# A recurrent block with routed experts on one core: smaller zero rows and prefetch before the slots, and a reordered first step

## What is computed

```
x = x + layernorm(attn(layernorm(x)))     # token shift, k/v/r projections, the wkv recurrence,
                                          # output projection, then a channel mix of width 1024
x = x + layernorm(ffn(layernorm(x)))

def wkv step(aa, bb, pp; k, v):           # per channel, along the tokens
    p  = max(pp, u + k);  y  = (exp(pp-p)*aa + exp(u+k-p)*v) / (exp(pp-p)*bb + exp(u+k-p))
    p2 = max(pp + w, k);  aa = exp(pp+w-p2)*aa + exp(k-p2)*v;  bb = exp(pp+w-p2)*bb + exp(k-p2)

def ffn(x):
    idx = argmax(x @ Wg)                  # one of 8 experts for each token
    return geglu(x, shared weights) + geglu(x, W1[idx], W2[idx], W3[idx])
```

## Time and profile before

| | |
|---|---|
| median of 3 runs | 1000.21 us (999.18 to 1000.51) |
| profiled execution | 1001.62 us, its span 999.7 us |
| TensorE busy | 924.4 us, 92% |
| VectorE busy | 725.1 us, 73% |
| GpSimd busy | 591.2 us, 59% |
| ScalarE busy | 586.2 us, 59% |
| chain that ended last | TensorE 64%, VectorE 11%, GpSimd 8%, no visible wait 7% |
| DMA | 152.09 MB, mean 152 GB/s |

### The profile page before, as it was taken

The page is one execution under the profiler, slowest core; times in us unless marked ns, Lnnn a source line. Parts: engine busy times, 40 slices in busy tenths (PEclk is TensorE's granted clock), DMA queues, the critical chain, the costliest instruction groups (busy, mean ns, idle before and its releaser), DMA issues.

```text
span 999.7 us, 27993 instructions
## 1 busy us (share of the span) xinstructions
PE 924.4 (92%) x9734; PEld 836.7 (84%) x9734; DVE 725.1 (73%) x1651; ACT 586.2 (59%) x1014; POOL 591.2 (59%) x800
## 2 busy tenths in 40 slices
PE   2477999999999999999999999869999999999994
PEld 1366888888888889888888878769999999999994
DVE  6999999999999999999999985614444444444442
ACT  5487768868868868869778755313333333333340
POOL 5475766866866866866866441434455555555553
PEclk9699999999999999999999999989999999999998
DMA  7033152152253153163171263936787778576410
GB/s 240 13 107 112 48 212 79 71 212 70 81 212 105 42 218 97 42 221 94 42 254 53 86 211 128 336 132 188 232 273 250 232 250 273 171 245 216 159 56 21
DMA packets 82091, 152.09 MB, mean 152 GB/s; under 512 B 5423, under 2 KB 62896, under 8 KB 76914
## 3 DMA queue, kind: packets, MB, share of 16 engines
q1 hardware_dynamic: 34528, 72.39, 21.1%
q10 hardware_dynamic: 42944, 61.98, 19.2%
q0 software_dynamic: 4560, 16.98, 4.4%
HBM read 183.59 MB, written 46.25 MB: 230 GB/s over the span
## 4 chain that ended last, share of the span: by engine, by line
PE 64%; DVE 11%; POOL 8%; issue 7%; ACTq 4%; DMA 3%; ACT 3%; SPq 1%; POOLq 0%; DVEq 0%
PE up L366 12%; PE up L368 12%; PE up L367 12%; PE yp L366 6%; PE yp L368 6%; PE yp L367 6%; PE yp L572 2%; PE yp L575 2%; PE tp L375 2%; ACTq L940 2%; PE yp L588 2%; DVE arena L1026 2%; POOL mix_s L1608 1%; DVE er L1127 1%; POOL routed_rows L1641 1%
## 5 line engine op out<-in xcount | busy, mean ns | idle before, releaser
L366 PE MATMUL up<-mix_s,arena 128*128 128x128 f16 x1248 | 211.9, 219 | 0.3 <-DVE ex L1474 0.2
L367 PE MATMUL up<-mix_s,arena 128*128 128x128 f16 x1248 | 211.8, 219 | 0.0
L368 PE MATMUL up<-mix_s,arena 128*128 128x128 f16 x1248 | 211.8, 219 | 0.0
L366 PE MATMUL up<-xf_s,arena 128*128 128x256 f16 x512 | 139.5, 272 | 1.5 <-issue 1.5
L1707 POOL TENSOR_TENSOR kf_s<-ex,kf_s 128x512 f16<-128x512 f32 x78 | 90.2, 1156 | 85.6 <-ACT kf_s L986 85.5
L368 PE MATMUL up<-xf_s,arena 128*128 128x256 f16 x512 | 139.5, 273 | 0.0
L367 PE MATMUL up<-xf_s,arena 128*128 128x256 f16 x512 | 139.5, 272 | 0.0
L1474 DVE SCALAR_TENSOR_TENSOR ex<-up,ex 128x512 f32<-128x512 f32 x78 | 53.9, 691 | 102.6 <-ACT ex L980 102.5
L366 PEld LDWEIGHTS up<-mix_s,arena 128*128 128x128 f16 x1248 | 122.4, 98 | 1.3 <-DVE ex L1474 1.2
L367 PEld LDWEIGHTS up<-mix_s,arena 128*128 128x128 f16 x1248 | 122.4, 98 | 0.4
L368 PEld LDWEIGHTS up<-mix_s,arena 128*128 128x128 f16 x1248 | 122.4, 98 | 0.0
(11 more groups left out here) (226 smaller groups left out, 2865.6 us busy)
## 6 DMA issues: line engine op xcount, KB each, us to landing
arena<-w_split ACTq DMA_DIRECT2D x113, 1024.0 KB
arena<-in_W SPq DMA_DIRECT2D x24, 1024.0 KB, 6.5
w_split<-arena SPq DMA_DIRECT2D x24, 1024.0 KB, 9.2
rows<-routed_rows ACTq DMA_DIRECT2D x39, 261.0 KB, 2.8
arena<-w_split SPq DMA_DIRECT2D x9, 1024.0 KB
normed<-routed_rows ACTq DMA_DIRECT2D x37, 128.0 KB, 2.5
x_in<-in_x SPq DMA_DIRECT2D x16, 256.0 KB, 2.8
x_res<-in_x SPq DMA_DIRECT2D x16, 256.0 KB, 2.8
```

Of the source, the lines that this page charges most:

```text
L366: pe.matmul(out, stat(0), mov(0), start=first, stop=False)
L367: pe.matmul(out, stat(0), mov(1), start=False, stop=False)
L368: return pe.matmul(out, stat(1), mov(0), start=False, stop=last)
```

## The change

In the passage: the zero tile has 520 columns (`ID`) in place of 780. SyncE writes the last 260 columns of all eight zero blocks before the first slots, and the first 520 of all eight behind them, under a semaphore of their own, for which ScalarE waits at the end of slot 0. ScalarE issues no zeros. Slot 1's up weights aren't prefetched; they are loaded once, without a condition, behind slot 1's rows, and TensorE's count for them is lower by one load. In the head: in step 0 the first exponential stands ahead of `above(1)`, and keep times values goes to `delta2`, a tile that is free in that step, without a wait for the last relu pieces. The low halves of pieces 4 and 5 move from step 1 to step 0, before `kept`, and that of piece 6 from `own(4)` to `own(3)` of step 1.

```diff
-        zero_row = ex.rearrange("p n k c -> p (n k c)")[:, 2 * CT * CH:2 * CT * CH + ROW]
+        zero_row = ex.rearrange("p n k c -> p (n k c)")[:, 2 * CT * CH:2 * CT * CH + ID]
...
-        OWN_LO = {(-2, 0): (0, 3), (-1, 1): (3, 4), (1, 3): (4, 6), (1, 4): (6, 7), (2, 3): (7, 8), (2, 0): (8, 9)}
+        OWN_LO = {(-2, 0): (0, 3), (-1, 1): (3, 4), (0, 4): (4, 6), (1, 3): (6, 7), (2, 3): (7, 8), (2, 0): (8, 9)}
...
-                for e in range(E // 2):
+                for e in range(E):
                     at = sp.value_load(end_at[0:1, e:e + 1], min_val=0, max_val=E * REGION - P)
-                    sp.dma_start(routed_rows[bass.ds(at, P)], zero_row).then_inc(S("zeroed"), 16)
+                    sp.dma_start(routed_rows[bass.ds(at, P), ID:ROW], zero_row[:, 0:ROW - ID]).then_inc(S("zeroed"), 16)
+
+            def other_zeros_at_ends():
+
+                for e in range(E):
+                    at = sp.value_load(end_at[0:1, e:e + 1], min_val=0, max_val=E * REGION - P)
+                    sp.dma_start(routed_rows[bass.ds(at, P), 0:ID], zero_row).then_inc(S("zeroed_rest"), 16)
...
-                for m in range(3):
-                    sp.wait_ge(S(f"expert_out{m}"), 16 * E)
-                for part in range(2):
-                    sp.dma_start(half(expert_w[1][:, 0:2], part),
-                                 half(w_split[0, :, 0:2], part)).then_inc(S(f"slot_w{part}_1"), 16)
...
+                    if n == 1:
+                        for m in range(3):
+                            sp.wait_ge(S(f"expert_out{m}"), 16 * E)
                     for part in range(2):
-                        sp.wait_ge(S(f"slot_w{part}_{n}"), 16)
-                        sp.dma_start(half(expert_w[n][:, 0:2], part), up_halves(e, part),
-                                     cond=e != 0).then_inc(S(f"slot_w{part}_{n}"), 16)
+                        if n == 0:
+                            sp.wait_ge(S(f"slot_w{part}_0"), 16)
+                            sp.dma_start(half(expert_w[0][:, 0:2], part), up_halves(e, part),
+                                         cond=e != 0).then_inc(S(f"slot_w{part}_0"), 16)
+                        else:
+                            sp.dma_start(half(expert_w[1][:, 0:2], part),
+                                         up_halves(e, part)).then_inc(S(f"slot_w{part}_1"), 16)
...
                     first_slots()
+                    other_zeros_at_ends()
...
-                        wait(pe, S(f"slot_w{q}_{b}"), 16 * (h + 2))
+                        wait(pe, S(f"slot_w{q}_{b}"), 16 * (h + 2 - b))
...
+                if at_step(i, 0):
+                    exps(0)
                 if not at_step(i, 1):
                     above(1)
...
-                exps(0)
+                if not at_step(i, 0):
+                    exps(0)
...
-                zeros_at_end(E // 2)
-                zeros_at_end(E // 2 + 1)
...
-                zeros_at_end(E // 2 + 2)
-                zeros_at_end(E // 2 + 3)
...
                         act.wait_ge(S("scattered_rest"), 16 * TT * 2)
+                        act.wait_ge(S("zeroed_rest"), 16 * E)
...
-                wait(dve, S("above"), 8 * (c + 1))
-                dve.tensor_tensor(dist[:], ex[:, E_KEEP], val[:], ALU.mult).then_inc(S("kept"), 1)
+                if at_step(c, 0):
+                    dve.tensor_tensor(delta2[:], ex[:, E_KEEP], val[:], ALU.mult).then_inc(S("kept"), 1)
+                else:
+                    wait(dve, S("above"), 8 * (c + 1))
+                    dve.tensor_tensor(dist[:], ex[:, E_KEEP], val[:], ALU.mult).then_inc(S("kept"), 1)
...
-                                           data1=dist[:, k, :], initial=aa[:, k, 0:1], op0=ALU.mult,
+                                           data1=(delta2 if at_step(c, 0) else dist)[:, k, :], initial=aa[:, k, 0:1], op0=ALU.mult,
```

More of the change, by code:

```diff
@@ L832, in own @@
                         own_hi(n)
[L834 to L839, removed]
                 def late_hi():
```

## The result

The changed kernel takes **1002.23 us** (median of 9 runs, 1001.01 to 1003.71), the kernel before in the same session 999.18 (9 runs). The ratio is 1.0026, with a 95% interval of 1.0015 to 1.0037: it is slower by a quarter of a per cent, where 997.5 us and a gain were forecast. The profiled execution of the changed kernel took 1002.23 us.

A forecast was written before the change was run, and what follows sets the result against it. VectorE was taken to bound up to about 110 us, then TensorE, except in the passage. Step 0 +1.95, step 1 -0.4, passage -7.85 + 3.6 gave -2.7 us from the median 1000.21: 997.5, range 993.5 to 1002.5.

The forecast's parts named there:

- the clock: Passage: full clock expected with under 2 us of standing before the first slot; 1.7 us of gain lost if it falls.
- Passage, first part: First slot's rows arrive earlier and its half-clock work goes, so slot 2 starts 7.85 us sooner.
- Slot 1's weights: Passage: loaded behind slot 1's rows, they land with 2 us to spare; priced at nothing, 1 us if slow.
- The rest of the zeros: Passage: eight transfers behind the slots land at 669.6, and TensorE stands 3.6 us before slot 2; bounds 0 and 9.8.
- 4.8 us from the landing to slot 1's product: Passage: slot 1's first product is out 4.8 us after the last zeros land, at 674.4.
- rival 3: Passage: late zeros hold ScalarE and reopen the hole at slot 2, clock falling; slower, 1004.0 us; chance 15%.
- Head: Step 0: a low half in VectorE's hole holds GpSimd's chain until about 31.2; +1.95 us, between -0.94 and +3.
- Step 1: Head: VectorE has one low half less but waits for the exponentials; -0.4 us, between -0.2 and -1.5.
- Rule on several engines: Passage: moving four zero transfers from ScalarE to SyncE costs issue periods alone, as all queues share 16 DMA engines.

The follow-up runs named there:

- mean of six: Mean over profiles of the kernel before, e1, e4, e5, e6 and e9, same passage: 104.5 us from the last chunk's division to the fifth transpose pair.
- e3: Passage edits alone against the kernel before, with the rest of the zeros issued earlier by ScalarE instead of SyncE: 996.09 us, ratio 0.9955.
- e2: Passage edits alone, head as before, against the kernel before: 1000.87 us, ratio 1.0009.
- e8: Kernel before with only the prefetch of slot 1's weights removed, zeros in whole rows as before: 996.15 us, ratio 0.9958.
- e10: Passage edits against the kernel before, with four of the eight rest-of-zeros transfers by ScalarE and four by SyncE: 997.75 us, ratio 0.9966.
- e7: Passage edits with split zeros but slot 1's prefetch and conditional load put back, against the kernel before: 996.46 us, ratio 0.9965.
- e4: Head edits alone against the kernel before, with the key weight's low half in eight operations of 256 columns: 998.83 us, ratio 0.9986.
- e6: Only the moved low halves of the head edits, against the kernel before: 1000.44 us, ratio 1.0007.
- e1: Head edits alone, passage as before, against the kernel before: 1001.89 us, ratio 1.0013.
- e11: Changed kernel with rest of zeros issued by ScalarE and the key weight's low half in eight operations, against the kernel before: 993.53 us, ratio 0.9927.
- e9: Only the moved low halves, the key weight's in eight operations, against the kernel before: 998.78 us, ratio 0.9986.
- e5: Only the earlier exponentials and the other product tile in step 0, against the kernel before: 999.53 us, ratio 0.9992.

## Why the prediction was wrong, point by point

**Mechanisms.** Each of them is in the trace, with its place: the product earlier and GpSimd's chain held in step 0; VectorE's wait in step 1 (1.86 us, "about 1.8"); SyncE's zero wait (1.4, "under 3"); the first pair at 654.52 ("near 654 plus the head's shift"); ScalarE standing at slot 0's end and TensorE before slot 2. The sign came out wrong by sizes: of the passage's terms each was off to the same side, and one, the clock, stood at nothing.

**Passage, first part: right in kind, over by about 2.** Forecast -7.85 at slot 2. The fourth pair (the prediction calls it the third) came at 672.22 instead of 678.29, -6.1; the passage began +1.2 late from the head, so -7.3 is the passage's own by this pair of profiles. The kernel before was caught with a late passage, though: against the mean of six it is -6.0, with the 1.1 of late weights within that, and e3 gives 4.5 by its ratio.

**Slot 1's weights: priced at nothing, cost 1.08** (1.97 in e2, 0.98 to 1.15 in e3, e8 and e10). The step took 2.6 us a megabyte at the full rate of 404 GB/s from an issue at 655.7; the issue was at 656.25, the rate was 338 to 384 GB/s, and product and wait show the second half there at about 666.9 where 663.2 was forecast. The text had the 1 us as its bound.

**The rest of the zeros: the step that failed.** Forecast landed 669.6, stall 3.6, nothing behind it; measured a stall of 4.65 and 2.8 of slow work, 7.5 in all, and this decided the sign. The rule "4.8 us from the landing to slot 1's product" was exact (672.44 to 677.25). The landing was not: the last issue came at 668.19 for 667.1, and landing took 4.25 for 2.5. What failed is the phrase "by then only these zeros are in the queues": it summed issues one by one, though the row of the full system allowed a sum of bytes. (Its 1.6 us for a period in full queues is also less than the 2.05 between the four old issues; the eight new ones came 1.45 apart, so that did no harm.) From 656 to 671 the changed kernel moved 4.9 MB: 2.1 of slot 1's weights, 2.1 of zeros and about 0.7 of scattered and gathered rows, at 338 to 384 GB/s between 658 and 670. By an estimate made afterwards that is 13.2 us at 370 GB/s, from 657 to 670.2, and 2.1 us of a last landing make 672.3. e7, without the 2 MB, shows the other case: landed at 668.8, with the issues as limit. TensorE was itself 1.8 us later than forecast (head and weights), so of the 2.84 us of later landing one reached the stall: 4.65.

**The clock: left out of the forecast, 2.8 us,** more than the 1.05 by which the stall was mis-sized. It stood in rival 3 alone, priced from a stall over the 5.96 us of before. What the runs show: stalls of 1.52 (e7) and 2.24 us (e10) with a clock of 1.00 behind them; 1.97 and 3.02 (e2) and 4.65 (changed kernel) with work at the lower level behind, which lost 1.8, 1.8 and 2.8 us. As 1.97 had it and 2.24 had not, the length of a stall alone doesn't tell, and one row can't say from where on the clock falls; I had used it as if it did.

**Head: right in kind, low by 0.7 in step 0.** Forecast +1.95 with the chain's end at 31.2; measured +2.62 and 32.15. The rule of the Trainium skill (SBUF — State Buffer, section "SBUF: two separate sides"), that the later of the two engines blocks for the whole instruction, is borne out at the first operation (2.24 us beside 2.28) and by e4. The forecast carried step 1's total over instead of walking the nine operations: those that start beside a wide VectorE operation are held as well. Step 1: forecast -0.4, measured -0.3 at its division. That the total of +1.55 is near the +1.2 of the last chunk is luck: steps 0 and 1 cost 2.3, and what came back later came back in kernels with the old head as well.

**The sum.** By the two profiles: +1.2 from the head at the end of the chunks, -7.3, +7.5, so +1.4 at slot 3, and +0.8 at the end. Against the mean of the six: +1.2, -6.0, +7.5, so 2.7, near the ratio's 2.6. By their ratios the two halves cost 0.13% and 0.09%. The forecast was -2.7; its rival 3 (1004.0, from a landing at 672.3 on) is the case that came in kind, and the landing, 672.44, was where it begins, though the stall was 4.65 and not the 6.3 that the prediction's sum gives for that landing, as TensorE itself came late. It had 15%, on the ground that the queues hold 4 MB by then in place of 9; 4.9 MB were enough.

**Rule on several engines.** The Trainium skill (Trainium Kernel Development and Optimization, Key Constraints) says that more issuing engines only save the sequencer's issue time. e2 and e3 show the two ways side by side: 4.8 us, with the same bytes. The traces don't contradict the rule, but show what issue time can be worth: the zeros needn't stand behind slot 1's 2 MB nor be issued after them; for a transfer that someone waits for, "only issue time" can be the whole gain.

**What stays open.** Between the divisions of step 1 and step 2 the changed kernel wins 1.3 us back (+2.33 to +1.01), and e6 loses 0.5 there. In these 37 us the granted clock falls in each profile, at another place and for another time (0.86 and 0.80 at 75 to 85 us before; 0.66 at 85 to 90 after; 0.72, 0.50 and 0.75 at 75 to 90 in e6). The six profiles with the old head take 35.7 to 37.5 us from the one division to the other, the changed kernel 35.7 and e6 37.5, so neither need be an effect of the edits. At the last chunk the six stand between 579.96 and 582.10, and the changed kernel's 581.95 and e1's 581.90 are within that; only e4 (578.73) and e11 (578.95) and, less, e9 (579.63) are outside. So the head's price at the end (0.13%, from its interval nothing to 0.27%) is less sure than its price in step 0. Why TensorE comes to the values at another time in each profile, and what decides when the clock falls, no run here shows.

## What to carry to other kernels

Before a transfer is put behind another in one queue, add up the bytes that stand in all queues from that moment to the time when someone waits for the last of them, and divide by the rate of a full stretch; take the later of that and of the issues' sum. When filling an engine's hole, look at what a second engine does in that hole: if that engine was seen to be held, cut the filler into small operations, or keep a rest behind it. And two edits that each gain may use up the same slack, as the split zeros and the late weights did: time them together and apart. Lastly, look at several profiles of the same part before an offset of a microsecond is put down to an edit.

## What the hardware showed that I had not expected

- GpSimd's chain of ten operations on 128x2 beside VectorE: 3.29 us with VectorE idle, 5.84 beside eight operations of 128x256 and what follows (e4), 8.67 beside one of 128x2048 and what follows (the changed kernel).
- It goes both ways. In e5 a VectorE product of 128x512 takes 1.69 us beside GpSimd's product, and 0.67 in the changed kernel, where GpSimd's product comes later:

```profile
29.17 1.27 POOL L1603 TENSOR_TENSOR mixed<-ex,val 128x512 f32<-128x512 f32 x1 [1.08 <-ACT ex L754]
29.30 1.69 DVE L1119 TENSOR_TENSOR mixed<-ex,state 128x512 f32<-128x512 f32 x1
```

- A register load in SyncE's queue took 0.27 us in quiet and up to 0.94 while weights were moved (1.11 before), so that a loop of loads and small transfers slows down just when it is to be hidden (eight issues: 8.82 us before the slots, 10.49 behind them).
